# Linear-attention layer on one core: the convolution on VectorE cut into halves of 256 columns

## What is computed

```python
def _causal_dwconv(x, w, b):          # KS = 4 taps, one filter per channel
    xc = jnp.transpose(x, (0, 2, 1))
    out = jax.lax.conv_general_dilated(xc, w[:, None, :], window_strides=(1,), padding=[(KS - 1, 0)], feature_group_count=xc.shape[1], ...)
    return jnp.transpose(out + b[None, :, None], (0, 2, 1))
q = jax.nn.silu(_causal_dwconv(x @ Wq, qcw, qcb))
k = jax.nn.silu(_causal_dwconv(x @ Wk, kcw, kcb))
v = jax.nn.silu(_causal_dwconv(x @ Wv, vcw, vcb))
def step(S, inps):                    # over the 2048 tokens, for each head
    qt, kt, vt, at, bt = inps
    err = jnp.einsum('bhvk,bhk->bhv', S, kt) - vt
    S = at[..., None, None] * S - bt[..., None, None] * (err[..., None] * kt[:, :, None, :])
    ot = jnp.einsum('bhvk,bhk->bhv', S, qt)
    return (S, ot)
```

## Time and profile before

| | before |
|---|---|
| time, median of 3 runs | 3634.66 us (3632.86 to 3637.85) |
| the profiled execution: its own time / its span | 3629.29 us / 3627.7 us |
| mean granted TensorE clock | 0.995 of full |
| busy PE / PEld / DVE / ACT / POOL | 98% / 81% / 66% / 64% / 55% |
| the 9 convolution instructions of a turn (L1254), all turns | 1152 of 748 ns, 861.6 us |
| DMA, mean | 100 GB/s |

### The profile page before, as it was taken

How to read it: one execution, slowest core, us unless ns; L and a number is a source line. 1 busy time by engine, 2 the same in 40 slices (tenths; PEclk the granted TensorE clock), 3 DMA queues, 4 the chain that set the end, 5 groups by cost and what they waited for, 6 DMA issues and landing times. The chain is left out here.

```text
span 3627.7 us, 105696 instructions
## 1 busy us (share of the span) xinstructions
PE 3540.8 (98%) x32416; PEld 2923.7 (81%) x32416; DVE 2393.3 (66%) x5749; ACT 2318.7 (64%) x6430; POOL 1986.7 (55%) x4917
## 2 busy tenths in 40 slices
PE   8999979999999999999999999999999999999999
PEld 6777757888888888888888888888888888877887
DVE  5544446777777777777777777777777777763222
ACT  3444337777777777777777777777777777763111
POOL 3444435666666666666666666666666666653000
PEclk9999989999999999999999999999999999999999
DMA  5543343333333333333443333333333333354543
GB/s 200 203 145 118 133 144 71 75 76 85 76 78 75 81 81 77 76 76 87 114 142 75 83 79 78 75 78 84 76 77 76 83 78 77 98 164 125 142 141 114
DMA packets 420912, 364.13 MB, mean 100 GB/s; under 512 B 190880, under 2 KB 321952, under 8 KB 414496
## 3 DMA queue, kind: packets, MB, share of 16 engines
q1 hardware_dynamic: 418304, 350.90, 35.8%
q0 software_dynamic: 2080, 6.82, 0.5%
HBM read 281.09 MB, written 76.55 MB: 99 GB/s over the span
## 5 line engine op out<-in xcount | busy, mean ns | idle before, releaser
L1254 DVE SCALAR_TENSOR_TENSOR conv<-bank,tap,conv 128x512 f32<-128x512 f32 x1152 | 861.6, 748 | 156.3 <-ACT conv L1390 127.9
L1080 POOL TENSOR_TENSOR prods<-Lb,Tc 128x60 f32<-128x60 f32 (+14 forms) x1920 | 482.2, 251 | 606.7 <-DMA Lb<-base_d 463.4
L1460 PE MATMUL bank<-hx_hi,w_hi 128*128 128x512 f32 x1536 | 663.4, 432 | 0.0
L1460 PE MATMUL bank<-hx_hi,w_lo 128*128 128x512 f32 x1536 | 644.4, 420 | 19.4 <-DVE Tnb L1216 18.1
L1460 PE MATMUL bank<-hx_lo,w_hi 128*128 128x512 f32 x1536 | 637.9, 415 | 0.0
L1087 POOL TENSOR_TENSOR Tc<-Tc,prods 128x56 f32<-128x56 f32 (+13 forms) x1792 | 459.1, 256 | 142.5 <-POOL prods L1080 3.8
L1371 ACT ACTIVATE Wc<-bank 128x128 f32<-128x128 f32 x512 | 141.1, 276 | 366.0 <-PE bank L1562 327.5
L1460 PEld LDWEIGHTS bank<-hx_hi,w_lo 128*128 128x128 f32 x1536 | 292.7, 191 | 58.2 <-DVE Tnb L1216 23.9
L1460 PEld LDWEIGHTS bank<-hx_hi,w_hi 128*128 128x128 f32 x1536 | 292.2, 190 | 36.4
L1208 DVE SCALAR_TENSOR_TENSOR S<-S,gamma,bank 128x128 f32<-128x128 f32 x480 | 167.1, 348 | 228.8 <-PE bank L1573 218.8
L1460 PEld LDWEIGHTS bank<-hx_lo,w_hi 128*128 128x128 f32 x1536 | 292.4, 190 | 29.4
(11 more groups left out here) (198 smaller groups left out, 8979.9 us busy)
## 6 DMA issues: line engine op xcount, KB each, us to landing
Lb<-base_d SPq DMA_DIRECT2D x128, 512.0 KB, 4.7
gamma<-gamma_d SPq DMA_DIRECT2D x128, 258.0 KB, 3.6
alpha<-alpha_d SPq DMA_DIRECT2D x128, 256.0 KB, 3.2
oT_d<-oG SPq DMA_DIRECT2D x128, 256.0 KB, 4.4
gu_raw<-in_gate_up SPq DMA_DIRECT2D x16, 1408.0 KB, 6.4
o_raw<-oT_d SPq DMA_DIRECT2D x13, 1024.0 KB, 6.8
w_raw<-oT_d SPq DMA_DIRECT2D x12, 1024.0 KB, 7.0
hx_hi<-xT_hi_d SPq DMA_DIRECT2D x9, 1024.0 KB, 7.4
```

What stands on the lines that cost most here:

```text
L1080: pool.tensor_tensor(prods[:, :, i + 1:], Lb[:, i, :, i + 1:], Tc[:, :, i:i + 1].to_broadcast([P, G, SB - 1 - i]), ALU.mult)\
L1254: dve.scalar_tensor_tensor(out=conv[i][:, to], in0=PJ[PJ_OF[g][i]][:], scalar=tap[:, i, j + 1:j + 2], in1=conv[i][:, to], op0=ALU.mult, op ...
L1460: last = pe.matmul(dst, a[:, i, k], b[:, k], start=(j == 0), stop=(j == 3 * KC - 1))
```

## The change

Each convolution instruction of 512 columns becomes two of 256. The first half stands at the old step; the second half is issued at the next step, ahead of the first half that may be due there, and behind the chain's S or R if one is due at that step. Only the second half adds to `conv_done`, and the first half keeps the wait that the whole had.

```diff
+                def conv_half(i, j, first):
+                    to = slice(KS - 2 - j + first, KS - 2 - j + first + GT // 2)
+                    return dve.scalar_tensor_tensor(out=conv[i][:, to], in0=PJ[PJ_OF[g][i]][:, first:first + GT // 2],
+                                                    scalar=tap[:, i, j + 1:j + 2], in1=conv[i][:, to],
+                                                    op0=ALU.mult, op1=ALU.add)
+
                 for s in range(STEPS):
...
+                    if proj and s - 1 in CONV_AT:
+                        conv_half(*CONV_AT[s - 1], GT // 2).then_inc(conv_done, 1)
                     if proj and s in CONV_AT:
                         i, j = CONV_AT[s]
                         if j == 0:
                             dve.wait_ge(tap_done, at(3, 4, i + 1))
                         else:
                             dve.wait_ge(conv_done, at(9, 4, 3 * i + j))
-                        to = slice(KS - 2 - j, KS - 2 - j + GT)
-                        dve.scalar_tensor_tensor(out=conv[i][:, to], in0=PJ[PJ_OF[g][i]][:],
-                                                 scalar=tap[:, i, j + 1:j + 2], in1=conv[i][:, to],
-                                                 op0=ALU.mult, op1=ALU.add).then_inc(conv_done, 1)
+                        conv_half(i, j, 0)
```

## The result

| | before | after |
|---|---|---|
| time, median of 5 runs each | 3632.86 us (3630.17 to 3637.85) | 3653.13 us (3652.01 to 3660.5) |
| ratio, after to before | | 1.0064 (95%: 1.005 to 1.0078) |
| the profiled execution: its own time / its span | 3629.29 / 3627.7 us | 3660.5 / 3658.9 us |
| mean granted TensorE clock | 0.995 | 0.994 |
| busy PE / PEld / DVE / ACT / POOL | 98 / 81 / 66 / 64 / 55% | 97 / 80 / 70 / 64 / 54% |

The change costs 20 us, 0.6%. The profiled execution of after is the longest of its five, and that of before is shorter than all five of its own, so their difference, 31 us, is too large: the medians say what the change costs, and the two traces only where. The stages before and after the heads are as long as they were, at the same clock.

The account below looks back on a forecast made before the run. PE's own stream was taken as the bound, POOL's circuit close behind. 1.26 us a head, partly given back, left +0.59, x31 = +18, less 1.5: about +16, so 3651 us, range 3636 to 3668.

Parts of the forecast that it names:

- What bounds the kernel: PE's own stream sets the time, 84.81 us a head alone; POOL's circuit is close at 85.4; DVE has room.
- The price of a half: On DVE a half takes 0.48 us; start to start 0.40, or 0.52 with the wait for `conv_done`.
- (a): Gate's projection, g = 3: PE waits for the last q convolution's second half, behind R of chunk 3; 0.57 us lost.
- signs of being wrong: R of chunk 3 right behind a half, DVE never idle before it; unchanged g = 3 turns; a lasting step-20 wait.
- (b): k convolution, each turn: the silu kT ends later, so PE's load L1627 goes 0.13 us later.
- R at +1.32: In the k convolution, R of chunk 1 starts 1.32 us behind the first half's start at 2028.06.
- (c): End of turn: late S of chunk 3 costs PE 0.11 us with g=0, 0.03 each with g=1 and 2.
- (d): R of chunk 1 goes 0.15 us earlier; PE gains only after the loop's jump back, -1.5 us; other delays hide.
- The sum and what is given back: 1.26 us a head, 39 us over 31 rounds; part replaces waits for Tnb, leaving +0.59 a head, about +16 us.
- Given back in full: Rival: the margins of (b) and (c) are nothing, PE needs no more than now: 3632 to 3641 us, 22%.
- nothing given back: Rival: POOL's circuit stretches with PE, so all 39 us stay: 3673 us, 12%.
- Faster: Rival: a shorter instruction ahead lets R go 0.15 us earlier at each PE wait for it: 3619 us, 4%.

Follow-up runs that it names:

- q alone: Only the three q convolutions halved and interleaved, k and v whole, against the kernel before: 3638.88 us, ratio 1.0018.
- k alone: Only the three k convolutions halved and interleaved, q and v whole, against the kernel before: 3641.64 us, ratio 1.0023.
- visit at 21: PE reads Tnb at step 21 instead of 20: on the kernel before 3620.82 us, on the changed kernel 3652.68 us.
- v alone: Only the three v convolutions halved and interleaved, q and k whole, against the kernel before: 3643.55 us, ratio 1.0031.

## Why the prediction was right

3651 us were forecast and 3653.13 came out. The change itself was forecast at +16 on 3634.66 and came out as +20 on 3632.86, so a part of the closeness is the start from a median that was 1.8 us too high. Slower was the likeliest by far, and the main mechanism is the one given. Step by step:

**What bounds the kernel: right.** DVE took 177 us more of work and stayed at 70%; every loss is a wait of PE for a late producer. I had put DVE at 72%, 240 us more: I added the durations of halves that overlap each other at their ends.

**The price of a half: right.** 0.48 us, and 0.40 and 0.52 as intervals; three in a row took 1.40.

**(a): right.** Load at 0.06 behind the half, 0.05 forecast; the floor of g = 3 longer by 0.54 with q alone, 0.57 forecast; 23 waits in 23 heads, 0.92 each for some 0.8. One of the signs of being wrong did come, an R of chunk 3 right behind a half with DVE not idle before it, and meant nothing: R is as far behind PE's L1555 as it was. The sign was badly chosen, since the prediction's own sum left only 0.10 of the 0.27 us idle.

**(b): right in its sum, wrong in its parts.** Forecast: 0.13 in each turn, 0.52 a head. Measured: 0.34 behind L1633 at g = 0, and 0.06 of floor in the three others (k alone), 0.52 a head. That the sums agree is luck. The step that failed is "R at +1.32". It holds with g = 1, 2 and 3. With g = 0, the very turn whose rows were read, R stays where it was, at +1.48, because two more waits stand behind its `chain_done`; so 0.16 isn't gained, the three halves behind it end later by that, and the kT starts 0.10 behind them where 0.04 was taken. The row couldn't tell: R followed 1.47 after 2028.06, and two whole intervals are 0.79 + 0.67 = 1.46, so it looked as if DVE's work alone had set it. The code could have told, which gives this R three waits. In the turns after the jump back, where R does come early, another margin is missing, the 0.2 us of cover ahead of kT. With g = 1, 2, 3 kT is 0.20 late where 0.25 was forecast, and the load 0.10 where it was 0.13.

**(c): right in kind, a little small.** 2.69 us to S against 2.71 forecast. The floors of g = 0 with the visit at 21 differ by 0.50, and without the 0.34 of (b) 0.16 is left; 0.11 was forecast. With g = 1 and 2 it is 0.02 (v alone) to 0.07 (0.13 less 0.06, visit at 21); 0.03 was forecast. What was missed is that this term is not given back, as v alone shows (its place is behind the visit), and that v alone costs two to three times what its late S explains.

**(d): right.** The wait for R after the jump back is gone: 8 waits and 1.6 us in the 2000; 1.5 in all was forecast.

**The sum and what is given back: right, with errors that cancel.** PE's own stream grew by 1.35 us a head, 1.26 forecast: 42 us for 39. Of the 39, 21 were to be given back and 22 of 42 were. But the parts differ. I took turn g = 3 as one that never loses time by Tnb, from the one round of the earlier trace rows; half of its turns do, 0.45 us each, at L1638. That loss isn't given back but grows: the mean of g = 3 lies 0.27 over its floor before and 0.40 after. What is given back is at g = 0, where PE's stream is 0.50 longer (21.77 less 21.27, visit at 21) and the mean only 0.07, so 0.43 for the 0.46 forecast; and at g = 2, where the mean doesn't grow and the stream does by 0.11. Together the two traces show 0.45 a head, 14 us, and the medians of the times 22. The traces can't account for the other 8: after's is the longest of its five executions. And the term of (c), which the sum treats like the others, isn't given back. To sum against before's own profiled time and add the difference to the median was right: had the forecast been read against the profiled execution of after, it would seem 9 us short.

**The rivals.** "Given back in full" falls, since the margins of (b) and (c) were all spent; "nothing given back" falls by the pair with the visit at 21, which shows what that would cost (32 us, and 42 by the floors). "Faster" falls too: R of chunk 3 is held by PE's L1555 and its wait is still 0.4 us 69 times. Of the rule it rested on (the Trainium skill, "Perfetto Trace Analysis", Optimizing Scalar/DVE Operations: break up an unsaturated engine's instructions where it makes others wait) the runs show the one place where it holds, (d), some 2 us over the ten jumps, and three where the opposite does.

## What to carry to other kernels

When an instruction is cut, ask two things of each cut: what now stands between the first part and the last, and who waits for the last. The reader of the whole result waits for the last part, so if anything at all is put between the parts, the result is later by that and by the fixed cost of one more instruction; only what stands in between can gain. A stall on the engine that bounds is cheap where a second circuit would have stopped that engine a little later anyway, and costs at least its full price behind that point. An instruction that waits for several semaphores pays for each wait that stands behind the late one, about 0.09 us here, so the late one should stand last. And before a margin is read off one round, look at all of them: half of the 30 turns of g = 3 had a wait that the one turn read didn't have.

## What was not expected of the hardware

Moving one wait of PE by one step of 38 gave before 13 us. The view of the waits names Tnb for only 6.7 us of 2000, and one would not look there. But with the visit at 21 the row "issue" of the same line falls too, from 11.6 to

```profile
PEld bank L1460 <- issue: 5.0, 17, 0.6
```

and the two rows together from 18.3 to 9.8. So a part of the wait for Tnb seems to be listed as "issue". For the long turns of g = 3 the sequencer's records show how: at L1638 `on_done` is met at 898.22, 0.04 behind the end of DVE's last `on`, the waits for two more semaphores follow, and the load goes at 898.40; the view puts all 0.32 of it down to "issue".

Two halves in a row on DVE take 0.88 us where the second needs nothing of the first (2055.04, place (c)) and 1.00 where it waits for it (2030.88, place (a)), with 0.48 for each alone: the one pair overlaps by 0.08, the other has a gap of 0.04. Durations can be added for the second kind alone, hence 177 us more of busy time and not 242 (2304 x 479 ns less 861.6).

The time from the start of a turn to Tnb falls into steps some 0.35 us apart, at places of its own for each g: in before near 10.0 and 10.3 with g = 3, near 10.1, 10.5 and 10.8 with g = 0. Nothing here explains these steps; it wasn't tried.
